# A two-layer AdaLN transformer on one core: loads in the order of use, the relative bias read mirrored, two attentions interleaved, layer 1's exponentials placed behind the router's

## What is computed

```python
mod = (silu(c) @ wmod).reshape(8, 6, 1, -1)         # sa, ca, ga, sb, cb, gb
ga = (2 * (ga >= 0) - 1) * maximum(abs(ga), 0.25)   # gb alike
h = layernorm(x) * (1 + ca) + sa;  x = x + ga * attention(h)
h = layernorm(x) * (1 + cb) + sb;  x = x + gb * ffn(h)

# layer 0 attention: 16 heads averaged to 4, with a relative position bias
scores = q @ mean(k).T + mean(compute_bias(rel_bias, N, N));  out = softmax(scores) @ mean(v)
# layer 0 ffn: 8 heads; per token and head one of 8 value and output experts, causal attention between
# layer 1 attention: for each token a 16 x 16 attention over its heads, keys with a position encoding
# layer 1 ffn: router softmax over 8 experts, each takes its 256 best tokens; gelu experts, gated sum
```

## Time and profile before

| | us |
|---|---|
| median of 3 runs | 850.14 (849.24 to 850.52) |
| profiled execution | 848.31 |
| its span, first to last instruction | 846.4 |
| granted TensorE clock, mean of the span | 0.982 of full |
| TensorE busy | 778.1 (92%) |
| VectorE busy | 551.8 (65%) |
| ScalarE busy | 388.5 (46%) |
| GpSimd busy | 185.4 (22%) |

### The profile page before, as it was taken

How to read it: one execution, slowest core, us unless ns; L and a number is a source line. 1 busy time by engine, 2 the same in 40 slices (tenths; PEclk the granted TensorE clock), 3 DMA queues, 4 the chain that set the end, 5 groups by cost and what they waited for, 6 DMA issues and landing times.

```text
span 846.4 us, 18617 instructions
## 1 busy us (share of the span) xinstructions
PE 778.1 (92%) x6621; PEld 584.0 (69%) x6621; DVE 551.8 (65%) x1634; ACT 388.5 (46%) x1056; POOL 185.4 (22%) x232
## 2 busy tenths in 40 slices
PE   5878999999998999899989998999899887999994
PEld 4645675775786577648765876587567766998994
DVE  4425749677675766586648674876776754354688
ACT  1464545445633563455345534641463335645431
POOL 0132212142106220621052115301320403000000
PEclk9989999999999999999999999999999998999998
DMA  7901002032040204020402040203202412000000
GB/s 225 371 27 47 5 1 52 25 76 52 3 101 1 52 0 99 1 51 0 99 1 51 0 99 1 51 2 101 51 2 57 144 51 52 1 0 1 7 19 25
DMA packets 54124, 42.40 MB, mean 50 GB/s; under 512 B 37868, under 2 KB 46844, under 8 KB 52648
## 3 DMA queue, kind: packets, MB, share of 16 engines
q1 hardware_dynamic: 54056, 41.58, 18.3%
HBM read 31.99 MB, written 9.58 MB: 49 GB/s over the span
## 4 chain that ended last, share of the span: by engine, by line
PE 43%; issue 32%; POOL 12%; DVE 9%; ACT 2%; POOLq 0%; DVEq 0%; DMA 0%; SPq 0%; ACTq 0%
PE ps L1375 6%; PE ps L1591 4%; PE ps L1451 4%; PE ps L1483 3%; PE ps L1580 3%; POOL wide L526 3%; POOL sc L512 3%; DVE shared L1167 2%; DVE shared L1160 2%; PE ps L1535 2%; POOL sc L504 2%; POOL wide L531 2%; PE ps L1550 2%; PE ps L1470 2%; PE ps L1361 2%
## 5 line engine op out<-in xcount | busy, mean ns | idle before, releaser
L1375 PE MATMUL ps<-veF,hB 128*128 128x512 f32 x256 | 123.2, 609 | 1.0 <-DVE shared L1028 0.9
L1028 DVE COPY_PREDICATED shared<-ghot,ps 128x512 f32<-128x512 int32 x128 | 88.3, 726 | 3.5 <-issue 1.2
L679 ACT ACTIVATE sc<-sc,nmax 128x128 f32<-128x128 f32 (+1 forms) x128 | 57.2, 447 | 63.4 <-DVE nmax L1014 62.9
L1375 PEld LDWEIGHTS ps<-veF,hB 128*128 128x128 f32 x256 | 44.7, 189 | 53.3 <-issue 34.4
L1451 PE MATMUL ps<-wide,oeF 128*128 128x256 f32 x256 | 66.2, 399 | 13.1 <-ACT lexp L762 13.1
L512 POOL TENSOR_TENSOR sc<-sc,rg 128x384 f32<-128x384 f32 x64 | 51.7, 829 | 72.0 <-DVE rg L1001 71.6
L1451 PE MATMUL ps<-early_masks,oeF 128*128 128x256 f32 x256 | 62.9, 385 | 3.4 <-issue 3.4
L1451 PEld LDWEIGHTS ps<-wide,oeF 128*128 128x128 f32 x256 | 47.6, 195 | 25.6 <-issue 17.2
L504 POOL TENSOR_TENSOR sc<-sc,rdenA 128x512 f32<-128x512 f32 x32 | 32.6, 1041 | 140.2 <-DVE rdenA L957 140.2
L1591 PE MATMUL ps<-oeF,wide 128*128 128x128 f32 x512 | 60.9, 277 | 1.5 <-DVE shared L1160 1.5
L1591 PEld LDWEIGHTS ps<-oeF,wide 128*128 128x128 f32 x512 | 59.2, 192 | 2.3 <-DVE shared L1160 1.9
(11 more groups left out here) (224 smaller groups left out, 1497.6 us busy)
## 6 DMA issues: line engine op xcount, KB each, us to landing
chosen<-hot_scratch SPq DMA_DIRECT2D x16, 512.0 KB, 5.8
v_scratch<-shared SPq DMA_DIRECT2D x16, 512.0 KB, 5.1
vg<-v_scratch SPq DMA_DIRECT2D x16, 512.0 KB, 5.2
veF<-in_L_ffn_value_experts SPq DMA_DIRECT2D x1, 2048.0 KB, 11.5
oeF<-in_L_ffn_output_experts SPq DMA_DIRECT2D x1, 2048.0 KB, 15.9
early<-in_L_attn_w_qkv SPq DMA_DIRECT2D x1, 1536.0 KB, 19.0
shared<-bias_scratch SPq DMA_DIRECT2D x2, 512.0 KB, 6.0
veF<-in_L_ffn_W SPq DMA_DIRECT2D x1, 1024.0 KB, 5.3
```

Source lines behind the costliest of these rows:

```text
L679: act.activation(v, v, ACT.Exp, bias=nmax[:, h % RING, t:t + 1], scale=-1.0, accum_out=denB[:, h * T + t:h * T + t + 1]).then_inc(s_("f_e" ...
L1028: dve.copy_predicated(val[:, t, :].rearrange("p (h k) -> p h k", h=HF), ghot[:, t * HF:(t + 1) * HF, e].bitcast(I32).unsqueeze(2) .broadca ...
L1375: pe.matmul(ps[:, vbank(j), :], tok(hB, t), veF[:, :].rearrange("p (h e k) -> p e h k", h=HF, e=EF)[:, e, :, :], start=True, stop=True).th ...
```

## The change

Four things are changed together.

1. SP's loads are in another order: c, ident, the bias's tables, wmod, x, then the four attention weights; `bo1`, `bsel`, `bqkvT` and `kpos` stand behind them, and the store and the reads of the bias come last. `flip` is not loaded.
2. The bias is written reversed by ACT, read from HBM with ascending offsets and reversed again by the read side of four ACT copies; PE has no part in it. Wq and Wk are summed over their groups by DVE and then transposed by PE; Wv and Wo are folded as before and come first. The modulation of the last four batches moves from ACT to DVE, and the normalised tiles are turned into banks 4 to 7 instead of 0 to 3. DVE takes its layer norm sums ahead of the modulation, and the additions for layer 1's keys (`keys_added`) behind N1 of batch 0.
3. The attentions of batches 0 and 1 are interleaved; their two head pairs use different banks, and the gate matmuls stand between them.
4. In `softmax`, EXPS moves from place 11 to place 12.

```diff
-            softmax = {"start": (ADDS,), 9: (MAXES,), 11: (EXPS,), 14: (SUMS,)}
+            softmax = {"start": (ADDS,), 9: (MAXES,), 12: (EXPS,), 14: (SUMS,)}
...
             attn0(0, 0, TAKE)
-            for n in whole_attn0:
+            for n in (QKV, S0, S1):
                 attn0(0, 0, n)
             attn0(1, 0, TAKE)
-            for n in (QKV, S0):
-                attn0(1, 0, n)
+            attn0(1, 0, QK)
+            gates(0, 0, GATE0)
+            for n in (N0, N1, T0, V0, T1):
+                attn0(0, 0, n)
+            attn0(1, 0, S0)
+            attn0(0, 0, V1)
+            attn0(0, 0, OUT)
+            attn0(1, 0, S1)
+            gates(0, 0, GATE1)
+            attn0(1, 0, VP)
             after_attn0(0, 0, PROJECT)
-            for n in (N0, S1):
+            for n in (N0, T0):
                 attn0(1, 0, n)
             after_attn0(0, 0, ADD)
-            for n in (T0, N1):
+            for n in (N1, V0):
                 attn0(1, 0, n)
             after_attn0(0, 0, NORM)
-            for n in (V0, T1, V1, OUT):
+            for n in (T1, V1):
                 attn0(1, 0, n)
             after_attn0(0, 0, MODULATE)
+            attn0(1, 0, OUT)
...
+        def early_batch(b):
+            return type(b) is int and b < AHEAD
+        def logits_bank0(b, p, hp):
+            return (4 + p if early_batch(b) else 4) + 2 * hp
+        def turned_bank0(b, hp):
+            return 5 + 2 * hp if early_batch(b) else 1 + hp
...
-                src = bass.AP(tensor=bias_dram.tensor, offset=N - P - t * P, ap=[[1, P], [512, KV0], [1, N]])
+                src = bass.AP(tensor=bias_dram.tensor, offset=1 + t * P, ap=[[1, P], [512, KV0], [1, N]])
...
+            act.wait_ge(s_("bias_in"), 32)
+            for h in range(KV0):
+                act.activation(bias0[:, h, :, :], biasR[:, h, :, ::-1], ACT.Copy).then_inc(s_("bias_ready"), 1)
+
             act.wait_ge(s_("mod_ready"), 1)
-            for b in range(B):
+            act.sem_inc(s_("n_h"), B)
+            for b in range(B // 2):
                 if b % 2 == 0:
                     act.wait_ge(s_("n_tr"), b // 2 + 1)
-                modulate(0, b, hE[:, b * N:(b + 1) * N], ps[:, b // 2, (b % 2) * N:(b % 2 + 1) * N])
-
-            for h in range(KV0):
-                act.wait_ge(s_("bias_p"), h + 1)
-                act.activation(bias0[:, h, :, :].rearrange("p t n -> p (t n)"), ps[:, 4 + h, :],
-                               ACT.Copy).then_inc(s_("bias_ready"), 1)
+                act.activation(hE[:, b * N:(b + 1) * N], ps[:, 4 + b // 2, (b % 2) * N:(b % 2 + 1) * N], ACT.Identity,
+                               bias=col(0, b), scale=col(1, b)).then_inc(s_("h_first"), 1)
...
+            for i in range(2):
+                w = wraw[i].rearrange("p c n -> p (c n)")
+                loaded(dve, ("wq", "wk")[i])
+                link(dve.tensor_tensor(w[:, 0:512], w[:, 0:512], w[:, 512:1024], ALU.add))
+                dve.tensor_tensor(w[:, 0:256], w[:, 0:256], w[:, 256:512], ALU.add).then_inc(s_("w_sum"), 1)
...
+            for b in range(B // 2, B):
+                if b % 2 == 0:
+                    dve.wait_ge(s_("n_tr"), b // 2 + 1)
+                dve.tensor_scalar(hE[:, b * N:(b + 1) * N], ps[:, 4 + b // 2, (b % 2) * N:(b % 2 + 1) * N], mod[:, 1, b:b + 1],
+                                  mod[:, 0, b:b + 1], ALU.mult, ALU.add).then_inc(s_("h_second"), 1)
...
-            for i in range(4):
-
-                loaded(pe, ("wq", "wk", "wv", "wo")[i])
-                for m in range(2):
-                    for g in range(G0):
-                        mm = pe.matmul(ps[:, i, m * P:(m + 1) * P], wraw[i][:, 2 * g + m, :], ident[:, :],
-                                       start=(g == 0), stop=(g == G0 - 1))
-                mm.then_inc(s_("w_tr"), 1)
...
                     if p == 0:
                         wait_apart(pe, (s_("a_qs"), b + 1), (s_("a_ks"), b + 1))
-                    else:
+                        if early_batch(b):
+                            pe.wait_ge(s_("h_first"), B // 2)
+                            pe.wait_ge(s_("h_second"), B // 2)
+                    elif not early_batch(b):
                         pe.wait_ge(s_("a_sc"), b * 8 + 4)
...
                 if n == PROJECT:
                     normed(k)
+                    if type(b) is int and b == 0:
+                        pe.wait_ge(s_("gate1"), 2)
                     pe.wait_ge(s_("a_ots"), b + 1)
```

152 lines of the change are left out of this document (84 added, 68 removed).

## The result

| | before | after |
|---|---|---|
| median of the runs (range) | 849.9 us (849.2 to 850.5) | 834.5 us (831.9 to 836.7) |
| ratio to before, 95% interval | | 0.983 (0.980 to 0.985) |
| profiled execution; its span | 848.3; 846.4 | 833.8; 832.0 |
| mean granted clock | 0.982 | 0.977 |

Faster by 15 us, but 11 us above the forecast of 823.3 and above its range. The page's busy times answer to the earlier trace rows: TensorE has 6 us less of work, and the span is 14.4 shorter.

The account below looks back on a forecast made before the run. It took TensorE, busy for 92% of the span, as the bound, with gains only where it stands still or runs at the lower clock; 16.6 + 10.2 = 26.8 us off the median of 850.1 gave 823.3 us, range 817.5 to 828.

Parts of the forecast that it names:

- Part 1: Product loop, exponentials at place 12: waits gone, clock gained, a little given back; 16.6 us, between 10 and 17.7.
- The five waits: Product loop: TensorE's waits for the router's exponentials all fall, 13.1 us.
- the low stretches behind the gap: After the product loop's idle gap TensorE runs partly at 1.2 GHz; three times 1.5, 4.5 us, bounds 0 and 4.6.
- One thing is given back: Jump to the loop's head: early TensorE meets late VectorE at `gone`; costs 1.0 us, bounds 0 and 3.
- The prediction's own sign of being wrong: Loop: the forecast is wrong if rounds are not 3 to 4 us shorter, 83.06 between the products before.
- Part 2: Opening up to the first attention: less TensorE work, first projection at 26.3, 10.6 us before 36.90.
- Free of the bias it would be 25.5: Opening: the first projection's start if the bias load, landing at 22.8, did not set it.
- rival (c): Opening: costly mirrored bias copies make the kernel slower, from 7.3 us apiece; 853 us at 8 apiece; chance 0.02.
- Part 3: First two attentions interleaved: 31.1 us to first values against 32.7, plus 2.0 of low clock, so 0.4 worse.
- The opening as a whole: Start to first layer's values: 10.6 - 0.4 = 10.2 us won, between 6 and 13.
- (b): Loop: the wait is replaced, later sums make VectorE jump back late; 12.6 us back, 836; chance 0.07.
- (a): Loop and opening: the clock doesn't pay, taking back 4.5 and 2 to 4 us; 830.8 us; chance 0.20.

Follow-up runs that it names:

- e_place_only: Kernel before with one number changed, layer 1's exponentials at place 12 of the product loop instead of 11: 831.6 us, ratio 0.981.
- e_two: Changed kernel with two rounds in each passage of the loop, so one jump back in place of three: 828.5 us, ratio 0.976.
- e_bias_early: Changed kernel with the bias store issued behind Wk and the mirrored reads behind Wo, ahead of the small loads: 834.4 us, ratio 0.984.
- e_pad_244: Changed kernel with 244 idle instructions more for VectorE, the head of its loop at instruction 820 instead of 576: 824.5 us, ratio 0.973.
- e_pad_bias: Changed kernel with 4 idle VectorE instructions ahead of the loop, bias store behind Wk and mirrored reads behind Wo: 823.8 us, ratio 0.972.

## Why the prediction was wrong

**Part 1, waits and clock: right, and a little small.** The five waits fell, the router's pair starts early (259.42, products without a gap from 258.97), and the low stretches behind the gap are gone. Forecast 13.1 + 4.5 = 17.6 us; the product passages became 19.5 shorter. e_place_only, this part alone, gave 17.4 us against 16.6 forecast.

**Part 1, "One thing is given back": the step that failed.** It took 1.0 us (its parts, 0.6 twice less 0.3, make 0.9), bounds 0 and 3; the profile says 9.4. In e_place_only, with the loop where it was, the same term is 2.0 (136.95 against 134.95 for the three values), inside the bounds: the forecast missed that the opening would move the code. The number came from the right place, `gone` 2.83 us after the last reciprocal in the earlier trace rows, and was read as the price of a jump. It was the arrival of the first of two pieces of code. The second piece showed in the same timeline, in a row that I hadn't used, the kernel before's `geq` in that round:

```profile
362.46 0.29 DVE L987 TENSOR_TENSOR geq<-gsig,gtop 128x128 f32<-128x128 f32 x1 [0.65 <-DVE gtop L985]
```

That is 5.0 us after the last reciprocal ended (357.24 and 0.20). Seven instructions more in the opening, which the forecast costed as VectorE's time and found hidden, moved `gone` behind the same border. Each of three holds then costs 2.9 us of waiting and about 1 us of clock. The prediction's own sign of being wrong appears: from projection to projection the rounds behind a jump take 82.0 to 82.1 us, against 81.5 to 83.9 before, and not 3 to 4 less. With the loop moved by four instructions (e_pad8) the changed kernel takes 821.1 us, 2.2 below the forecast. That this is so near is partly luck: in its profile the six passages win 22.1 against the 16.6 of part 1, the opening 7.7 against 10.2, and 3.2 are lost behind the last projection, which the forecast didn't have.

**Part 2, first projection: forecast 26.3, measured 28.69, 27.6 to 29.6 in the other profiles.** The step that failed here is the landing of the loads. TensorE's folds start with Wv, at 18.23 and not at 15.3:

```profile
18.23 5.39 PE L1279 MATMUL ps<-ident,wide 128*128 128x128 f32 x32 [4.56 <-DMA wide<-in_L_attn_Wv]
```

The four weights were issued from 4.96 to 14.48, since SyncE's queue took 4.65 us to issue Wq (its row is in the chain's stretch, 4.96 to 9.61) and 1.4 to 1.7 for each of the others, where I had counted a rate and no issue. The bias was in at 25.5, beyond my bound of 25. "Free of the bias it would be 25.5" stays open: e_bias_early was free of it and started at 27.64, but it had the new wait for `bo1`. The four mirrored copies took 2.19 us in all, 2.2 forecast; rival (c) needed 7.3 for each.

**Part 3: right in its length, wrong in where the clock's cost ends.** From first projection to first values 33.3, forecast 33.1, 2.0 of low clock among it. But the low clock lasted into the first passage, which lost 1.7. The opening as a whole brought 5.9 by the profiles and 4.3 alone by the medians, forecast 10.2, bounds 6 and 13.

**Behind the last projection** 2.0 us more, in the same instructions. 1.2 of them lie behind TensorE's stop of 8.24 us for GpSimd (8.38 before), from the first transposes to the experts' first matmuls: 9.69 us against 8.47. The clock stays at its lower level there for longer:

```profile
688.00:694.00 6.00, 6.00 (x72) 5.19 (x72) 1.54 (x3) 1.95 (x4) 1.56 (x2) 0.51 0.01 3
```

The whole stretch took from 249.5 (e_place_only, as before) to 254.0 us (e_two) in the profiles of these kernels, over the same instructions; I can't attribute it to the change.

**The rivals.** (b) named the right place, VectorE late at the jump and TensorE held for what it had won, at 12.6 back and 836; its reason (late sums) was wrong: the sums ended at 264.6, 0.9 after the projection began, 0.5 by the forecast, and in e_pad8 `gone` follows such sums after 1.84 us. Its chance of 0.07 was set by a row that hid the second piece. (a) took place in the opening only: behind the products the clock stayed at 1.00 until VectorE's hold.

## What to carry to other kernels

When an engine's first instruction behind a jump is idle for "issue", count the instruction transfers on the page of the profile, and read the next instructions as well: each short idle time behind it can be a further piece of code that arrives, and an edit anywhere ahead of the loop can move the costly instruction behind a border. The releaser that a row names can be an old one: the kernel before's 2.83 us stand there as a wait for `gexp`. If a hardware loop is somewhat shorter than what stays at hand, move it by a few idle instructions, or write it out, and compare the timelines before judging an edit by its time. A wait that is hidden behind another one is free only as long as the other one stands.

## What the runs showed of the hardware

- VectorE's code comes in transfers of 8 KB, 128 instructions each. With a loop of 274 instructions that reaches into a fourth piece there are five for each jump, three of them at the jump, 2.4 us apart in the changed kernel; VectorE is held until 2.8 to 3.0 us after its last reciprocal for the piece with the loop's head and 5.1 to 5.5 us for the next (5.9 in e_two). With three pieces there are none, and no hold (1.84, its data's time). Four idle instructions are worth 13 us here.
- The granted clock at the first projection: behind 2.36 us without matmuls it is 0.57 in 28 to 32 us, and the four matmuls take 2.08 us (changed kernel); behind 1.82 us it is 1.00 in that window, and they take 1.13 (e_pad8). Both have the same transposes ahead of it. The length of the gap alone doesn't decide it: behind 2.44 us it is 1.00 as well, and they take 1.13 (e_pad_244).
- A mirrored read on ScalarE costs no more than a plain one: 617 ns for 512 columns from SBUF, as mean of four, against 653 for the kernel before's plain bias copies from PSUM (median of four).
- The same GpSimd copy of 256 columns took 0.40 us alone, and beside VectorE's normalisations 1.93 in e_bias_early but 0.40 in e_pad_bias.
- SyncE's queue needs 1.4 to 4.7 us to issue one 512 KB load when others are in flight.
